# Second turned copy of the feed-forward rows on GpSimd instead of ScalarE, with new stage orders on four engines, in a small language-model tower on one Trainium2 core

## What is computed

```
x  = emb[tokens] * sqrt(128) + pos
s  = sum_d scale_d * tanh(q[:, :, None, :] + k[:, None, :, :])   # additive attention, 96 x 96 x 128 tanh a sequence
x1 = layer_norm(x + softmax(s) @ v @ Wo + bo) * g1 + beta1
h  = layer_norm(x1 + relu(x1 @ W1 + bf1) @ W2 + bf2) * g2 + beta2
h  = h + causal attention with 8 heads of _layernorm(h)
h  = h + mixture of 64 experts (2 a token) of _layernorm(h), a shared expert, and a last feed-forward
```

## Time and profile before

| what | us |
|---|---|
| median of the three runs | 824.73 |
| the profiled execution | 828.12 |
| its span in the trace | 826.1 |
| start of the first pair's first `add` | 25.27 |
| start of the fifth pair's first `add` | 131.49 |
| start of the sixteenth pair's first `add` | 476.93 |
| end of the last `add` | 505.48 |
| first load of expert weights | 590.71 |

### The profile page before, as it was taken

One profiled execution on the slowest core, in us unless ns is written; L12 is line 12 of the kernel. 1 busy time (PEld: TensorE's weight loads), 2 busy tenths in 40 slices (PEclk: granted clock), 3 DMA queues, 4 the chain that ended last, 5 costly groups with the idle time before them and its releaser, 6 DMA issues.

```text
span 826.1 us, 21375 instructions
## 1 busy us (share of the span) xinstructions
PE 742.8 (90%) x7238; PEld 600.6 (73%) x7238; DVE 622.6 (75%) x1635; ACT 623.8 (76%) x1471; POOL 353.2 (43%) x466
## 2 busy tenths in 40 slices
PE   0656799999999999999999999987789999999898
PEld 0533567777777677677677677765679999999787
DVE  0699999999999999999999996543423435443685
ACT  0477899999999999999999999764235556665354
POOL 3101223444644544554544543666126545555111
PEclk9988999999999999999999999998889999999999
DMA  3940000000000000000000000000299999994511
GB/s 82 261 93 6 7 2 7 14 13 12 18 14 11 16 16 12 16 16 11 16 16 12 11 16 7 16 15 25 88 342 393 376 394 401 320 359 160 160 32 38
DMA packets 50096, 78.99 MB, mean 96 GB/s; under 512 B 7428, under 2 KB 34203, under 8 KB 50000
## 3 DMA queue, kind: packets, MB, share of 16 engines
q1 hardware_dynamic: 33824, 65.01, 22.9%
q0 software_dynamic: 5664, 7.92, 3.5%
q10 hardware_dynamic: 10512, 4.83, 2.1%
HBM read 63.95 MB, written 15.92 MB: 97 GB/s over the span
## 4 chain that ended last, share of the span: by engine, by line
DVE 45%; PE 33%; issue 11%; POOL 3%; ACT 2%; SPq 2%; DMA 2%; ACTq 1%; POOLq 0%; DVEq 0%
DVE arena L939 27%; PE big L1693 9%; PE b_qk L1704 4%; PE b_s L1704 4%; DVE mx L1069 3%; PE big L1749 3%; SPq L404 2%; PE b_s L1762 2%; DVE stat_h L982 1%; PE b_qk L1762 1%; DVE stat_x L982 1%; POOL rows_dram L616 1%; PE big L1496 1%; PE b_s L1383 1%; PE b_t L1686 1%
## 5 line engine op out<-in xcount | busy, mean ns | idle before, releaser
L939 DVE TENSOR_TENSOR arena<-qT,b_qk 128x2304 f32<-128x2304 f32 x128 | 323.2, 2540 | 3.4 <-PE b_s L1383 3.2
L683 ACT ACTIVATE arena<-arena 128x2304 f32<-128x2304 f32 x128 | 272.4, 2133 | 10.3 <-DVE arena L939 10.2
L1383 PE MATMUL b_s<-arena,apad 128*32 128x192 f32 x3072 | 149.6, 333 | 4.2 <-ACT arena L683 3.5
L846 ACT ACTIVATE act_h<-big,arena 128x128 f32<-128x128 f32 x324 | 92.7, 369 | 71.9 <-PE big L1693 66.1
L1383 PEld LDWEIGHTS b_s<-arena,apad 128*32 128x32 f32 x3072 | 89.5, 111 | 48.3 <-issue 13.8
L651 POOL DMA_INDIRECT eo_dram<-gT,toff x81 | 79.8, 985 | 96.6 <-DVE gT L1268 92.9
L579 POOL TENSOR_TENSOR kept<-kept,rs 96x384 f32<-96x384 f32 x64 | 52.7, 824 | 120.7 <-DVE rs L1075 120.5
L1693 PE MATMUL big<-hbT,arena 128*128 128x128 f32 x648 | 87.2, 278 | 1.6 <-DVE hbT L1257 1.6
L747 ACT ACTIVATE kept<-big,mx 96x96 f32<-96x96 f32 x256 | 83.5, 350 | 2.6 <-DVE mx L1069 2.6
L1693 PEld LDWEIGHTS big<-hbT,arena 128*128 128x128 f32 x648 | 80.1, 194 | 2.0 <-issue 1.3
L616 POOL DMA_INDIRECT rows_dram<-rows_now,slots x64 | 61.4, 960 | 42.8 <-DVE slots L1123 30.2
(11 more groups left out here) (227 smaller groups left out, 1410.8 us busy)
## 6 DMA issues: line engine op xcount, KB each, us to landing
arena<-in_wpack SPq DMA_DIRECT2D x81, 578.0 KB, 10.0
prT<-rows_dram ACTq DMA_DIRECT2D x73, 64.5 KB
rows_dram<-act_h SPq DMA_DIRECT2D x1, 4128.0 KB, 23.4
arena<-eo_dram SPq DMA_DIRECT2D x4, 512.0 KB, 7.4
x_dram<-res SPq DMA_DIRECT2D x16, 96.0 KB, 1.7
out<-of SPq DMA_DIRECT2D x12, 128.0 KB, 1.8
eo_dram<-gT,toff POOLq DMA_INDIRECT x81, 5.6
rows_dram<-rows_now,slots POOLq DMA_INDIRECT x64, 2.3
```

The source lines that it names most:

```text
L683: act.activation(v, v, ACT.Tanh).then_inc(s["tanh"], 1)
L846: last = act.activation(act_h[:, i, c * TILE:(c + 1) * TILE], big[i][:, c * TILE:(c + 1) * TILE], ACT.Silu, bias=wslot[:, slot, 2 * DFF + ...
L939: dve.tensor_tensor(ring[c % TRING].rearrange("p (x m n) -> p x m n", m=CQ, n=N), qv.unsqueeze(3).to_broadcast([D, SPLIT * QG, CQ, N]), kv ...
L1383: last = pe.matmul(b_s[32 * a:32 * a + 32, 0:SPLIT * N], apad[:, 31 - line:63 - line], t[:, :, a, m, :], start=(line == 0), stop=(line == ...
```

## The change

`x1T_affine` on ACT makes only x1T and signals the bank's release with it; GpSimd makes x1bT from x1T, as x1T + bf2 (`x1_bias`). DVE's small sum beta1 + bf2 goes. PE's `ffn1` waits for the bank's release, which now tells of x1T, and `ffn2` for GpSimd's copy.

```
-        b1f2 = sb("b1f2", [D, 1])
...
+            def x1_bias(p):
+                wait(pool, s["y2"], p)
+                pool.wait_ge(s["t_ev"], T_USE["x1_turn", p] + 1)
+                pool.tensor_scalar(x1bT[:, :], x1T[:, :], bf2, None, ALU.add).then_inc(s["x1bT"], 1)
...
-                act.activation(x1T[:, :], b_t[:, 0:TN], ACT.Identity, bias=beta1, scale=g1).then_inc(s["x1T"], 1)
-                act.activation(x1bT[:, :], b_t[:, 0:TN], ACT.Identity, bias=b1f2[:, :], scale=g1)\
-                    .then_inc(s["t_ev"], 1)
+                act.activation(x1T[:, :], b_t[:, 0:TN], ACT.Identity, bias=beta1, scale=g1).then_inc(s["t_ev"], 1)
...
-            dve.tensor_tensor(b1f2[:, :], beta1, bf2, ALU.add)
...
             def ffn1(p, k):
                 dst = big_bank(p, f"ffn1 {k}")
-                pe.wait_ge(s["x1T"], p + 1)
+                pe.wait_ge(s["t_ev"], T_USE["x1_turn", p] + 1)
...
             def ffn2(p):
                 wait(pe, s["ya_ev"], YA_USE["ffn2", p])
-                pe.wait_ge(s["t_ev"], T_USE["x1_turn", p] + 1)
+                pe.wait_ge(s["x1bT"], p + 1)
```

Every `body(n)` is written in another order, with the tables of PSUM uses to match. Three of the changed lines (DVE, PE, PE):

```
-                at(n, -1, setup)
+                at(n, 1, setup)
...
-                at(n, 1, products)
+                at(n, 2, products)
...
-                at(n, -1, setup)
+                at(n, 1, setup)
```

More of the change, by code:

```diff
@@ L75 @@
 YA_ORDER = [
-    (2, "attend1"), (1, "v_rows"), (5, "logits"), (5, "ranks"), (2, "ffn2"),
+    (3, "ffn2"), (2, "attend1"), (5, "logits"), (1, "v_rows"), (5, "ranks"),
 ]
@@ L825, in body @@
                 at(n, 3, exp2, 2)
-                at(n, 4, tn_rows)
+                at(n, 0, tanh, 2)
+                at(n, 3, exp2, 3)
+                at(n, 3, prT_copy, 1)
+                at(n, 4, hT_affine)
+                at(n, 3, mean_copy, 0)
+                at(n, 3, prT_copy, 2)
+                at_end(n, 5, silu_shared, 0)
+                at_end(n, 6, silu_shared, 1)
+                at(n, 0, tanh, 3)
+                at(n, 3, mean_copy, 1)
+                at(n, 3, prT_copy, 3)
@@ L828, in _ @@
+                at(n, 0, tanh, 4)
+                at(n, 2, xaT_copy)
+                at(n, 3, mean_copy, 2)
+                at(n, 0, tanh, 5)
+                at(n, 3, mean_copy, 3)
+                at(n, 2, g_copy, 0)
+                at(n, 1, products)
+                at(n, -1, xT_copy)
             act.wait_ge(s["ld_a"], 16 * 5)
@@ L1175, in body @@
-                at(n, 2, inv_sums, 0)
-                at_end(n, 6, shared_rows, 0)
-                at(n, 3, h1_stats)
-                at(n, 0, softmax1_max)
-                at_end(n, 6, shared_rows, 1)
+                at(n, 4, inv_sums, 0)
+                at(n, 1, add, 1)
+                at(n, 5, variance, "h1")
+                at(n, 4, mask_max, 1)
+                at(n, 2, softmax1_max)
+                at(n, 1, add, 2)
+                at(n, 3, x2_stats)
+                at(n, 5, h1_shift)
@@ new lines, in body @@
+                at(n, 3, means, "x2")
+                at(n, 2, p1T_copy)
+                at(n, 3, variance, "x2")
+                at(n, 4, mask_max, 2)
+                at(n, 4, inv_sums, 1)
+                at(n, 3, x2_rows)
+                at(n, 1, add, 3)
+                at(n, 4, mask_max, 3)
+                at(n, 3, x2_norm)
+                at(n, 2, x1_sums)
+                at(n, 4, inv_sums, 2)
+                at(n, 3, h0_stats)
+                at(n, 2, x1_rows)
+                at(n, 3, means, "h0")
@@ new lines, in body @@
+                at(n, 2, x1_stats)
+                at_end(n, 6, shared_rows, 0)
+                at(n, 3, variance, "h0")
+                at(n, 4, inv_sums, 3)
+                at(n, 1, add, 4)
+                at(n, 5, route)
+                at(n, 3, xa_norm)
+                at(n, 1, setup)
+                at(n, 1, add, 5)
+                at(n, 2, means, "x1")
+                at(n, 5, chosen)
+                at_end(n, 6, shared_rows, 1)
+                at(n, 0, x_rows)
+                at(n, 2, variance, "x1")
@@ L1181, in _ @@
+                at(n, 1, add, 6)
+                at(n, 2, x1_norm)
+                at(n, 5, one_hot)
+                at(n, 1, add, 7)
+                at(n, 3, mask_max, 0)
+                at(n, 5, ranks)
+                at(n, 4, h1_stats)
+                at(n, 0, queries)
+                at(n, 4, means, "h1")
+                at(n, 0, add, 0)
             in_turns(body)
@@ L1592, in body @@
             def body(n):
+                at(n, 4, pr_turn, 0)
+                at(n, 3, ffn2)
+                at(n, 2, p1_turn)
                 at_end(n, 5, shared1, 1)
-                at(n, 2, p1_turn)
-                at(n, 1, products)
+                at(n, 4, scores, 2)
                 at(n, 1, score, 0)
-                at(n, 4, heads_m, 0)
-                at(n, 1, score, 1)
-                at(n, -1, setup)
-                at_end(n, 6, shared2, 0)
-                at(n, 4, pr_turn, 1)
@@ L1617, in body @@
                 at(n, 3, xa_turn)
+                at(n, 4, attend2, 1)
+                at(n, 4, heads_m, 3)
                 at(n, 1, score, 4)
-                at(n, 4, pr_turn, 3)
                 at(n, 3, heads_g, 0)
+                at(n, 1, v_rows)
+                at(n, 0, xs_turn)
                 at(n, 3, heads_g, 1)
+                at(n, 3, heads_g, 2)
+                at(n, 2, x1_turn)
+                at(n, 3, scores, 0)
+                at(n, 4, attend2, 2)
                 at(n, 5, ranks)
-                at(n, 0, xs_turn)
@@ L1634, in body @@
                 at(n, 1, score, 7)
-                at(n, 2, ffn1, 0)
-                at(n, 2, ffn1, 1)
-                at(n, 3, scores, 1)
-                at_end(n, 4, shared1, 0)
-                at(n, 3, scores, 2)
-                at(n, 3, pr_turn, 0)
-                at(n, 2, ffn2)
             in_turns(body)
```

111 lines of the change are left out of this document (35 added, 76 removed), and 10 rows, old and new, of tables (BIG_ORDER, s).

## The result

The changed kernel took 802.29 us (median of 4 runs, 798.82 to 804.16) against 824.69 beside it (822.91 to 826.36): a ratio of 0.9718, interval 0.9696 to 0.974. The forecast was 798, within 789 to 813. So the medians differ by 22.4 us, 4.2 less than the sum of 26.6 that was forecast. The profiled execution took 801.53 with a span of 799.5, and its span is 26.6 us shorter than that of before.

A forecast was written before the change was run, and what follows sets the result against it. DVE alone was taken to set the steady turn, with waits deciding the first turn and the drain. Start -15.1, steady turns -9.6 and drain -1.9 sum to -26.6, from 824.73 to 798 us, range 789 to 813.

The forecast's parts named there:

- First `add`: Start: with `xs_turn` first on PE, DVE's first `add` starts at 12.6 instead of 25.27, 12.6 us earlier.
- First turn: First pair's turn: `setup` costs DVE 0.8, the 3.25 us wait for `score` goes, `qk`'s 1.81 stays; net -2.5 us.
- the two bounds: Start's gain: -11.8 if 3.25 us return in the second pair's turn, -16.9 if the `qk` wait is filled too.
- Steady turns: `grow` and `x_rows` on DVE, no longer beside a `normalise`, save 0.91 us a turn; 30.6 a turn, -9.6 in all.
- PE is a soft limit: Steady turns: PE's 30.74 us holds modelled ends, so the turn was taken as 30.6 rather than DVE's 30.5.
- The moved copy: ACT to GpSimd: ACT loses 0.39 us a turn, GpSimd's copy takes about 0.66 (0.44 to 0.84); cost nothing.
- Drain: After the last `add`: GpSimd's root of x2 no longer waits behind scatters, 0.6 us in three rounds, -1.9.
- the port: Rival, chance 0.09: GpSimd's copy stalls DVE instructions with two SBUF inputs, up to 0.66 us a turn, 8 us; 806.
- The turn keeps its length: Rival, chance 0.16: PE or mutual waits between two engines hold steady turns, so the 9.6 us are lost; 808.
- The longer drain: Rival, chance 0.07: each of three rounds after the last `add` takes 3 us longer in the new order; 809.
- the start held back: Rival, chance 0.05: a later `add` waits for `setup`'s constants or PE's late weights, losing all that was won; 811.
- PE held at the top of its turn: Rival, chance 0.05: PE's list waits for GpSimd's `normalise` and copy, delaying the fifth `add`; at 12 us held, 834.

The follow-up runs named there:

- b_start: Kernel before with only the start's stages moved: `setup` later on PE, DVE and GpSimd, `products` a turn later on PE; 809.24 us against 825.26, ratio 0.9801.
- b_apart: Kernel before with only two DVE stages moved, `h1_shift` behind add 3 and `x_rows` behind add 5; 819.57 us against 825.26, ratio 0.9929.
- b_copy: Kernel before in its old order, with only the second turned copy moved from ACT to GpSimd; 826.08 us against 825.26, ratio 1.0013.
- a_gpnorm: Changed kernel with `x1_norm`'s two instructions moved from DVE to GpSimd, behind its root of x1; 804.27 us, ratio 0.9747.

## Why the prediction was right, and where it was not

- **First `add`.** Forecast 12.6, measured 12.56. The step (PE turns the rows when they are there, the rest of the hand-over as before) held; the last digits are luck, since kernels with the old start began at 25.27 and 24.84 and those with the new one between 12.32 and 12.78.
- **First turn.** Forecast -2.5, measured -2.95. `setup` cost DVE 0.66 against 0.8, the wait for `score` went, that for `qk` stayed (1.54).
- **Turns 2 to 4.** The step that failed: "Net for the first turn ..., and for the start -15.1" has no term for the following turns, and they give back 2.86, so that the start is worth 12.8. It lies between the two bounds, but the mechanism given for the lower one (`products` in the second pair's turn) was not it: DVE has no wait for `score` in that turn, as the prediction said. What came instead is in the timelines above. In the second turn `x1_norm` no longer fills the wait for `qk` (0.5 of 0.73), and in the fourth DVE waits 2.30 us for PE where it waited 0.65 (1.65 of 1.93), 0.59 of it for `score`, against the mark "no DVE idle for `score` in the first turns". The clock is not the difference: `qk` took 1.65 us in the first two turns of the kernel before, too. Why PE is late there was not tried. It has 328 matmuls in the fourth turn where before and b_start have 318, and in the drain 487 where before has 502, so the new order may do some of the drain's work in the fill.
- **Steady turns.** Forecast 30.6, measured 30.58; -9.6 against -9.39. The first half of the reason (two instructions beside `normalise`) is shown by b_apart, and the sizes were right (0.91 together, 0.89 measured). That the turn could take 0.82 of the 0.89 was right because `h1_shift` and `x1_rows` still cover DVE's own dependence, which the prediction did not see. "PE is a soft limit" was half right: PE's work alone does not hold the turn at 30.55, but a loop through PE and ACT does, as far as the runs show, about 0.1 us above DVE's own list. That the loop came out no longer than this was not foreseen and is luck.
- **The moved copy.** Forecast nothing, shown by two runs in both orders. Its length was 0.77 us, 0.66 was estimated, within the bounds. ACT's turn fell to 29.87, 30.1 was forecast.
- **Drain.** Forecast -1.9, measured -3.75. The wait of the root for scatters went, as the prediction said, and 1.4 us are won up to the last pair's `heads_g`, though only two roots of x2, not three, lie behind the last `add`. (It is the first pair of `scatter_rows` that now follows `roots_h1` and stands ahead of this root; the second, which stood there, now follows the last `normalise`.) The 2.3 behind it had no term, and no run shows their cause. They belong to the new order: b_start and b_apart, with the old order of the drain, have it as long as before within a microsecond (92.5 and 93.7 us from the last `add` to the first expert matmul, 92.9 before, 89.0 after).
- **Rivals.** The copy meeting DVE ("the port", 0.09) did not come: in b_copy the `add` took 2515 to 2555 ns with a median of 2542, as before, and the steady turn 31.40 us. But all that ran on DVE beside the copy in the changed kernel was `add` (2.54 to 2.55 us each) and `mask_max` (0.54 to 0.55), which read PSUM. No DVE instruction with two inputs from SBUF met the copy, as `x_rows` and `grow` met a `normalise` in the kernel before (0.83 and 0.62 us, while `h0_stats`, with one input from SBUF, took 0.46 for its two instructions beside one and 0.48 at 90.60 us with none). So how long such an instruction would stand beside the copy, for which the forecast took up to 0.66 us, is not shown. "The turn keeps its length" came in part, as the loop that would take back the next gain. The longer drain, the start held back and PE held at the top of its turn did not come.

The forecast of the median, 798, was 4.2 too low. In the two traces the sum comes out to the tenth only because a start too large by 2.3 was made up for by a drain too small by 1.9 and a rest that is 0.7 shorter though nothing in it was changed, and because the profiled execution of before was a long one. Of the marks it named, the second pair came at 35.35 (36), the last `add` ended at 483.29 (480), and the first expert load followed after 81.48 (85 or less).

## What to carry to other kernels

Take a large reordering apart by what each stretch of the span gained: four stages of the start gave 16 of 23 us, two DVE stages another 6, and the edit in the title none. Before moving a small stage, look at what it separates: it may be the cover of a dependence between its neighbours (0.49 us from start to start here, against 0.38 with the stage between). When three engines are within half a microsecond of the turn, do not name one as the bound from its busy share; add work in one place and take it away in another, and see which places count. A row of PE without idle time can hide a wait: here the row of its weight loads shows one of 0.45 us at `o_begin`.

## What the runs showed of the hardware that was not expected

- GpSimd's `tensor_scalar` on 96 x 128 took 438 to 451 ns with multiply and add by two columns (`residual` in the changed kernel), but 785 to 1068 (median 810) with subtract and multiply by two columns (`x1_norm` in a_gpnorm). The last pair, with DVE idle beside it, took 807 and 787; those above 1000 ran beside DVE's `one_hot`.
- Behind a pair of DVE statistics instructions, an instruction that reads their result started 0.49 us after the first of them (b_apart), and one that does not 0.38 us after (before).
- Matmuls whose results nobody reads made the kernel faster (797.32 and 797.43 against 802.44 us). In the turns this is the granted clock, 1.00 instead of 0.50, at a `qk` for which DVE waits (0.9 us instead of 1.6).
